# Self-attention heads of a decoder layer pair: rounded three-part projections, a new order within a head's round, a transposed output

## The reference

```python
qkv = x @ qkv_w + qkv_b
q, k, v = jnp.split(qkv, 3, axis=-1)
q, k, v = (to_heads(q), to_heads(k), to_heads(v))          # 16 heads of 128
scores = jnp.einsum('bhid,bhjd->bhij', q, k) + _alibi_mask(s, NUM_HEADS)[None]
attn = jax.nn.softmax(scores, axis=-1)
ctx = jnp.einsum('bhij,bhjd->bhid', attn, v)
ctx = ctx.transpose(0, 2, 1, 3).reshape(b, s, NUM_HEADS * HEAD_SIZE)
return ctx @ out_w + out_b
```

## Time and profile before

| | |
|---|---|
| median of 3 runs | 554.89 us (551.62 to 555.03) |
| the profiled execution | 554.23 us, span from first to last instruction 552.6 us |
| busy TensorE / DVE / ACT / POOL | 519.9 / 338.3 / 300.3 / 4.1 us |
| mean granted clock of TensorE | 0.981 |
| from the start to head 0's turned weights | 25.6 us |
| a head's round | 8.78 us |
| turned weights of head 14 to the first cross scores | 23.5 us |

### The profile page before, as it was taken

How to read it: one execution, slowest core, us unless ns; L and a number is a source line. 1 busy time by engine, 2 the same in 40 slices (tenths; PEclk the granted TensorE clock), 3 DMA queues, 4 the chain that set the end, 5 groups by cost and what they waited for, 6 DMA issues and landing times.

```text
span 552.6 us, 16184 instructions
## 1 busy us (share of the span) xinstructions
PE 519.9 (94%) x7064; PEld 411.5 (74%) x7070; DVE 338.3 (61%) x757; ACT 300.3 (54%) x523; POOL 4.1 (1%) x12
## 2 busy tenths in 40 slices
PE   7999999999978999999999999899999899887896
PEld 6677777878757888887787887688877688645565
DVE  3243754765334775557475668765678774688971
ACT  2354464443415756666767557865656765454242
POOL 1000000000001000000000000000000000000000
PEclk8999999999979999999999999999999999979999
DMA  7912122121320112111121111111101110000000
GB/s 266 377 39 77 41 75 62 55 76 40 134 114 1 39 46 71 41 41 39 45 71 40 41 39 39 39 40 39 39 20 31 38 41 2 4 1 10 0 1 17
DMA packets 10791, 30.83 MB, mean 56 GB/s; under 512 B 1377, under 2 KB 4450, under 8 KB 9954
## 3 DMA queue, kind: packets, MB, share of 16 engines
q1 hardware_dynamic: 10274, 29.07, 15.9%
q0 software_dynamic: 192, 0.51, 0.3%
q10 hardware_dynamic: 256, 0.23, 0.1%
HBM read 29.35 MB, written 0.46 MB: 54 GB/s over the span
## 4 chain that ended last, share of the span: by engine, by line
PE 72%; DVE 13%; ACT 9%; issue 4%; DMA 2%; SPq 0%; DVEq 0%; ACTq 0%
PE psb L1219 10%; PE psb L1229 10%; PE psa L1151 8%; PE psa L1271 7%; PE psb L1289 5%; PE pst L1166 5%; PE psa L1159 5%; PE psb L1195 3%; PE psa L1175 2%; ACT shared L520 2%; PE pst L1437 2%; DMA cst<-consts_dram 1%; PE psb L1186 1%; PE psa L1437 1%; PE pst L1355 1%
## 5 line engine op out<-in xcount | busy, mean ns | idle before, releaser
L1219 PE MATMUL psb<-cx,wkv 128*128 128x500 f32 x288 | 78.5, 408 | 4.0 <-ACT vmem L371 4.0
L1229 PE MATMUL psb<-wkv,cx 128*125 128x256 f32 x552 | 77.4, 289 | 3.6 <-ACT kx L364 3.6
L1229 PEld LDWEIGHTS psb<-wkv,cx 128*125 128x125 f32 x552 | 68.3, 186 | 7.6 <-ACT kx L364 6.1
L1219 PEld LDWEIGHTS psb<-cx,wkv 128*128 128x128 f32 x288 | 51.0, 189 | 16.9 <-ACT vmem L371 4.5
L371 ACT ACTIVATE vmem<-psb 125x512 f32<-125x512 f32 x46 | 27.4, 596 | 57.5 <-PE psb L1229 57.5
L1271 PE MATMUL psa<-qb,kx 32*125 32x112 f32 x1536 | 54.7, 279 | 1.4 <-ACT vmem L371 0.8
L811 DVE TENSOR_SCALAR shared<-shared,top 125x896 f32<-125x896 f32 x48 | 30.8, 684 | 39.9 <-ACT shared L520 39.7
L313 ACT ACTIVATE shared<-shared,negmax 112x112 f32<-112x112 f32 x64 | 24.0, 376 | 55.0 <-DVE negmax L727 55.0
L1151 PE MATMUL psa<-xnT,whd 128*128 128x448 f32 x128 | 52.9, 558 | 0.8 <-ACT xnT L289 0.8
L1271 PEld LDWEIGHTS psa<-qb,kx 32*125 32x125 f32 x1536 | 46.3, 183 | 9.6 <-issue 4.8
L811 DVE TENSOR_SCALAR smem<-smem,top 125x896 f32<-125x896 f32 x48 | 30.8, 684 | 27.7 <-ACT smem L520 27.5
(11 more groups left out here) (298 smaller groups left out, 796.5 us busy)
## 6 DMA issues: line engine op xcount, KB each, us to landing
ring<-ctx_t_dram SPq DMA_DIRECT2D x24, 500.0 KB, 3.7
whd<-heads_dram SPq DMA_DIRECT2D x16, 385.0 KB, 3.2
whd<-heads_dram SPq DMA_DIRECT2D x16, 129.0 KB, 2.4
wraw<-w_dram SPq DMA_DIRECT2D x2, 1024.0 KB, 6.2
mats_sb<-mats_dram SPq DMA_DIRECT2D x1, 1536.0 KB, 14.9
wraw<-gate_dram SPq DMA_DIRECT2D x1, 1024.0 KB, 8.4
wraw<-up_dram SPq DMA_DIRECT2D x1, 1024.0 KB, 10.5
wraw<-down_dram SPq DMA_DIRECT2D x1, 1024.0 KB, 12.5
```

Of the source, the lines that this page charges most:

```text
L1219: last = nc.tensor.matmul(bank[:, 0:UT], wkv[a][:, 0, c, m * P:(m + 1) * P], cx[b][u % 2][:, c, :], start=(a == b and c == 0), stop=(a == ...
L1229: last = nc.tensor.matmul(bank[0:CT, t * D:(t + 1) * D], cx[b][u % 2][:, c, a0:a0 + CT], wkv[a][:, 1, c, :], start=(a == b and c == 0), st ...
```

## The change

- The projections of queries, keys and values are made of rounded products in three parts, as in the cross attention. ACT rounds a head's weights (`split_qk`, `split_v`) into `cq[HI]` and `wkv[HI]`, DVE makes the remainders (`rest_qk`, `rest_v`). The input is split once, into `x0[HI]` and `x0[LO]`. These buffers are those that the cross attention uses later.
- Values are projected for two heads at a time (256 columns), half of the tiles in each round.
- The weights are loaded as separate arrays (`wqk`, `wvp`, `wo`, and one `hb` for all biases and slopes), queries and keys up to five heads ahead, and the large loads are issued one a round in the head loop.
- A round on TensorE is now: turn of the divided weights of head h, scores of head h+1, attended values of head h, queries and keys of head h+2, values, output of head h. The division of head h+1 is done in round h.
- The output is summed with its features on the partitions (2 products of 448 columns a head). Its bias is added when it is copied to `yT`, and `turn_y` turns it back, one tile ahead of the cross attention and three in its first steps.
- ACT's and DVE's work between the heads is moved to other rounds, ACT's now at the end of a round, behind the splits. The load of the constants is cut in two, and POOL's loads wait for the input's normalisation.

The core of the diff:

```diff
+PARTS0 = ((HI, HI), (LO, HI), (HI, LO))
...
+            def split_qk(h):
+                act.wait_ge(s_w[h % 2], 16 * (h // 2) + 16)
+                if h >= 2:
+                    act.wait_ge(s_q, 2 * h - 2)
+                nc.scalar.activation(cq[HI][h % 2], whd[h % 2][:, 0:QW], ACT.Copy).then_inc(s_wh, 1)
...
             for h in range(H0):
-                head(h)
...
+                move_pT(h)
...
+                if h + 1 < H0:
+                    exps(h + 1)
...
+                if h + 2 < H0:
+                    move_qk(h + 2)
+                if h + 4 < H0:
+                    split_qk(h + 4)
+                if h % 2 == 0 and h // 2 + 2 < H0 // 2:
+                    split_v(h // 2 + 2)
...
+            def rest_qk(h):
+                dve.wait_ge(s_wh, h + 1)
+                nc.vector.tensor_tensor(cq[LO][h % 2], whd[h % 2][:, 0:QW], cq[HI][h % 2].bitcast(F32), ALU.subtract).then_inc(s_wl, 1)
...
             for h in range(H0):
-                head(h)
-                if h == 2:
+                if h + 1 < H0:
+                    masked(h + 1)
+                move_oT(h)
+                if h + 3 < H0:
+                    rest_qk(h + 3)
+                if h % 2 and (h + 3) // 2 < H0 // 2:
+                    rest_v((h + 3) // 2)
...
+                if h + 1 < H0:
+                    normalise_p(h + 1)
+                if h + 2 < H0:
+                    move_v(h + 2)
...
             def project_qk(h):
-                pe.wait_ge(s_w[h % 2], 16 * (h // 2) + 16)
+                pe.wait_ge(s_wl, h + 1)
                 for part in range(2):
                     if h:
                         pe.wait_ge(s_qe, 2 * h - 1 + part)
-                    for c in range(DC):
-                        last = nc.tensor.matmul(PS[0][:, part, 0:TOK], wq0(h, c, part), xnT[:, c, :], start=(c == 0), stop=(c == DC - 1))
+                    for a, b in PARTS0:
+                        for c in range(DC):
...
+                            last = nc.tensor.matmul(PS[0][:, part, 0:TOK], cq[a][h % 2][:, (c * 2 + part) * P:(c * 2 + part + 1) * P], x0[b][:, c, :],
+                                                    start=(a == b and c == 0), stop=(b == LO and c == DC - 1))
...
             def output(h):
+                pe.wait_ge(s_wo[h % 2], 16 * (h // 2) + 16)
                 pe.wait_ge(s_oe, h + 1)
-                for t in range(NT):
-                    last = nc.tensor.matmul(yrow(t), oT[:, t * TT:(t + 1) * TT], whd[h % 2][:, OB:OB + D], start=False,
-                                            stop=False, skip_group_check=True)
+                for m in range(DC):
+                    last = nc.tensor.matmul(pst[:, m, 0:TOK], whd[h % 2][:, QW + m * P:QW + (m + 1) * P], oT[:, :], start=(h == 0), stop=(h == H0 - 1))
...
+            scores0(0)
+            project_qk(1)
+            project_v(1)
+            for h in range(H0 - 1):
+                turn_pn(h)
+                scores0(h + 1)
+                attended0(h)
+                if h + 2 < H0:
+                    project_qk(h + 2)
+                    project_v(h + 2)
+                output(h)
```

More of the change, by code:

```diff
@@ L232, in _ @@
[L232 to L239, removed]
+            load_qk(1)
+            sp.dma_start(cst[:, P:], consts[:, P:]).then_inc(s_rest, 16)
@@ new lines, in _ @@
+            big = ((wraw[:, 0, :], gate, s_wff[0]), (wraw[:, 1, :], up, s_wff[1]), (wraw[:, 2, :], down, s_wff[2]),
+                   (mats_sb[:, :, :, :], mats, s_mats)) + tuple((ctxs[u], ctx_t[u], s_ctx[u]) for u in range(3))
+            for h in range(H0 - 2):
+                if h + 5 < H0:
+                    sp.wait_ge(s_wl, h + 4)
+                    load_qk(h + 5)
+                if h % 2 and (h + 7) // 2 < H0 // 2:
+                    sp.wait_ge(s_vl, (h + 5) // 2)
+                    load_v((h + 7) // 2)
+                sp.wait_ge(s_y, h + 1)
+                load_wo(h + 2)
+                if h < len(big):
+                    dst, src, landed = big[h]
+                    sp.dma_start(dst, src).then_inc(landed, 16)
@@ new lines, in project_qk, with project_v @@
+                    last.then_inc(s_q, 1)
+            def project_v(n):
+                j = n // 2
+                pe.wait_ge(s_vl, j + 1)
+                if n:
+                    pe.wait_ge(s_ve, n)
+                for i in range(2):
+                    t = 2 * (n % 2) + i
+                    for a, b in PARTS:
+                        for c in range(DC):
+                            last = nc.tensor.matmul(A2[0:TT, i * D:(i + 1) * D], x0[b][:, c, t * TT:(t + 1) * TT], wkv[a][:, j % 2, c, :],
+                                                    start=(a == b and c == 0), stop=(a == LO and c == DC - 1))
@@ L1248, in project_q, with turn_y @@
                 last.then_inc(s_qx, 1)
-            pe.wait_ge(s_wkv, 1)
+            def turn_y(t):
+                pe.wait_ge(s_ye, 1 + (t > 0))
+                pe.wait_ge(s_yed, 1 + (t > 0))
+                dst = T1 if t else A3
+                for c in range(DC):
+                    last = nc.tensor.transpose(dst[0:TT, c * P:(c + 1) * P], yT[:, c, t * TT:(t + 1) * TT], ident)
+                last.then_inc(s_yt, 1)
+            turn_pn(H0 - 1)
+            attended0(H0 - 1)
+            pe.wait_ge(s_wkv, 1)
+            project_k(0, 0, A0)
+            output(H0 - 1)
+            project_k(0, 1, A1)
+            pe.wait_ge(s_mask, H0)
+            turn_y(0)
+            project_vu(0, 0, kvb)
+            turn_x1(0)
             pe.wait_ge(s_mats, 32)
-            project_k(0, 0, kvb)
-            project_k(0, 1, pvb)
-            turn_x1(0)
-            project_vu(0, 0, A2)
             project_q(0)
-            project_vu(0, 1, A3)
+            project_vu(0, 1, pvb)
             def scores(pp):
```

312 lines of the change are left out of this document (181 added, 131 removed).

## The result

The changed kernel takes 526.35 us (median of 4, 525.77 to 528.47) against 554.19 beside it: a ratio of 0.953, 95% interval 0.950 to 0.957, or 27.8 us less.

The account below looks back on a forecast made before the run. TensorE's own work was taken to bound the head stage. Gains of 11.7 us (rounds), 3.9 (start) and 4.7 (tail) less 0.5 (later turns of y) summed to 19.8, taking 554.23 to 534.4 us, range 529 to 544.

Parts of the forecast that it names:

- Query and key projection 2.5 us, output 1.5: Per head round: 12 rounded 448-column products take 2.5 us instead of 3.01, two f32 output products 1.5 instead of 1.81.
- Values 1.52: Per head round: 12 rounded products of 256 columns take 1.52 us instead of 1.75 for 8 f32 of 128.
- Scores 0.9 and 0.1 for changes of kind: Per head round: scores take 0.9 us, and changes between kinds of product about 0.1, within a 7.8 us period.
- Waits behind ACT's weight passes 3.3: Head rounds: TensorE waits 0.6 to 0.8 us at the attended product in four rounds; with the weights' scale wait, 3.3 us.
- DVE's division off the path by 2 us, loads at nothing: Head rounds: divided weights ready at 5.7 us at the latest, wanted at 7.8; weight loads cost nothing.
- The start 3.9: Before the first turn of weights: it comes at 21.7 us instead of 25.59, a gain of 3.9, bounds 2 to 5.
- The tail 4.7: From turn 14 to the first cross scores: 18.8 us instead of 23.5, a gain of 4.7.
- A: Rival: ACT's copy of the turned weights comes 0.5 us late every round, 7 us lost, 541.5 us; chance 0.20.
- B: Rival: TensorE's clock falls to half in the tail behind short waits, costing 3.3 us, 537.7 us; chance 0.10.
- C: Rival: weight loads of the rounded projections not hidden, 0.074 us more per product, 27 us, so 562 us; chance 0.05.
- D: Rival: weight loads of the rounded projections quite hidden, 7.4 us better than summed, 527 us; chance 0.05.
- four signs of being wrong: 448-column product 0.23 us or more; first turn behind 23; rounds without weight pass wait for ACT; cross stage over 381 us.

Follow-up runs that it names:

- c1: The changed kernel run once more with nothing altered, beside other experiments on the same chip: 525.63 us.
- p3: The changed kernel with queries, keys and values made by 4 f32 products of the high parts each instead of 12 rounded, low parts left out: 540.62 us.
- o2: The changed kernel with the old order on TensorE and ACT, and DVE's remainders and between-head work behind the head's division: 543.87 us.
- a1: The changed kernel with six more ACT copies of 512 columns at the end of rounds 9, 10 and 11: 529.75 us.
- s3: The changed kernel with 10 instead of 18 products of the ones tile ahead of the start: 528.76 us.
- s4: The changed kernel with POOL's three loads going out at once, the constants still cut in two: 531.21 us.
- s1: The changed kernel with the constants loaded whole (188.5 KB) in one load where the identity columns alone stood: 527.26 us.

## Why the prediction was right in direction and short in size

The mechanism was right: TensorE's own list bounds the stage and got shorter. Three terms of the sum were too slow, and they are the steps that failed: the period of a round (7.8 for 7.55), ACT's weight passes (3.3 for 1.2), and the start, with the first projections put at half the clock (a gain of 3.9 for 7.2). Piece by piece:

- **TensorE bounds the head stage, so shorter products shorten it: right.** It is busy 106.5 of 107 us there in c1. The rounded products bring 15 us (p3).
- **Query and key projection 2.5 us, output 1.5: right** (2.55 and 1.50). A rounded product of 448 columns costs 0.2125, 0.026 over its columns; the forecast had 0.02.
- **Values 1.52: wrong by 0.12.** Twelve products of 256 columns take 1.40, 0.117 each. I took 0.127 from a whole group of the cross attention. Its weight loads have 125 columns and records of 0.188 us in the profile after, those of the heads' values 112 and 0.174; whether that makes the difference no run shows.
- **Scores 0.9 and 0.1 for changes of kind: wrong by 0.2.** Scores take 0.80 between two f32 groups. The 0.95 that I read the earlier trace rows was the distance to an output that needs DVE's bias, and I kept most of it. In the kernel before that bias ended at 144.93 and the output started at 144.99:

```profile
144.25 0.68 DVE L741 TENSOR_SCALAR vmem<-psb,whd 128x448 f32<-128x448 f32 x1 [0.19 <-PE psb L1195]
```

  The trace names no wait there, so this cause is read from the times. o2, where the output again stands behind the scores, has 1.03 from scores to output, and that is its 0.2 us more a round. Ahead of the first projection in the kernel before, with no bias to wait for, scores took 0.87. Next to nothing shows for changes of kind (attended 0.91 for 0.88). With the values and the rounding up to 7.8, the period was forecast 0.25 us too long, 3.5 us over 14 rounds. This is the largest single miss.
- **Waits behind ACT's weight passes 3.3: wrong.** The 14 rounds took 106.93, 1.2 over 14 periods, so 2.1 too much. The attended products come 0.15 to 0.35 us late in rounds 3, 5, 7 and 9, where I had 0.6 to 0.8 each, and some 0.4 lie about the weights' scale in rounds 5 and 6. I added whole records of ACT; a1 shows that their starts are to be added.
- **DVE's division off the path by 2 us, loads at nothing: right.** TensorE never waits for the division between turns 1 and 14, nor for a load behind the start.
- **The start 3.9: wrong, 7.0 to 7.2.** Against c1 the turn came 3.3 us sooner than forecast. 2.0 of it is the first projection, 2.6 us (9.52 to 12.14) where I had 4.6 at half the clock. I carried the half clock of the old start over, though the change removes the idle of 2.04 us that stood ahead of it, and that idle was in the earlier trace rows; s3 brings an idle of that length back, and with it 1.5 of the 2.0. Another 0.8 is the projection's start, with transposes from 7.6 to 7.8 on and not past 8; POOL's delay is what allows it (s4). The last 0.5 is values and scores.
- **The tail 4.7: right within 0.4 where the clock holds** (4.3 in c1); with the fall 3.3, and another 1.6 behind the first scores.
- **The three later turns of y 0.5: too much.** c1's last stretch is 0.1 us longer than before.
- **Rivals.** A (ACT late in every round) fell: in the plain rounds nothing waits. B came, in some executions, and cost 2.6 us. C (loads not hidden) fell: 24 products a round cost 3.95 us, of which 3.52 are their columns. The Trainium skill's rule that a load overlaps only products of other row groups ("TensorE: Matmul & The Clock Gate", Part 3, "The mechanism") isn't borne out here either: the values' loads have records of 0.174 us, longer than the pace of their products, 0.117. D named a time near the true one, 527, for a cause that is hardly there: over their columns the 24 products cost 0.43 us a round, where I had 0.48. That its number fits is luck.

The errors of the sum (3.5 + 2.1 + 3.3 + 0.4 less 0.4 for the tail: 8.9, which is c1's 28.7 - 19.8) all but one went one way: each doubtful piece was rounded to the slow side. The range left them no room below 529, and of the four signs of being wrong that I named none looks at the fast side, so none of them came.

## What to carry to other kernels

Sum an engine's list by the distances between starts, TensorE's and ACT's alike, and take a product's price from a place where nothing behind it waits. When a change takes away an idle spell of TensorE, price what comes behind it at the full clock as well, as a case of its own. A softmax's division can be kept out of TensorE's way by working one head ahead; in these runs that paid behind the last heads and in rounds that carry other work, and only while TensorE's own work is longer than the other engines' lists.

## What the runs showed of the hardware that I had not expected

- A 64 KB load that SP issued at 1.6 us, ahead of its weights, took 9.3 us to land with 496 KB of POOL's loads issued beside it, and 4.2 us without (s4). The whole 188.5 KB of constants in its place changed nothing (s1).
- At the start TensorE's clock fell to half behind idle spells of 2.04 us (s3) and 3.62 (s4) and didn't behind 0.49 (s1). It didn't fall at once: in s3 and s4 the eight transposes right behind the spell took 1.12 and 0.99 us at the full clock, and the projection behind them ran at half. In the kernel before, behind 2.04 us, the transposes were already at half (1.76 us). Behind the tail's spells of 1.3 and 0.5 us it fell in some executions of one and the same kernel and held in others.
- ACT's copies of 448 to 512 columns start 0.52 to 0.57 us apart with records of 0.62 to 0.64.
- Rounded products of 256 columns, each with its own weight load, follow each other every 0.117 us, though one load's record is 0.174.
